# Gated delta rule: output projection with exchanged operands, sums of squares with the squares as the moving operand

## The chip, the cores and the metric

The kernel runs on one core of one Trainium2 chip. The metric is the device time of one execution of the whole program in microseconds (us). TensorE, VectorE, ScalarE, GpSimd and SyncE (which issues the DMAs) each work through a queue of their own and wait for one another by semaphores. In the profile they are called PE (its loads of the stationary operand PEld), DVE, ACT, POOL and SP.

## What is computed

The program is a stack of eight blocks on 2048 tokens of 128 features. The change touches the first alone, the gated delta rule, with 16 heads, keys of 64 and values of 128 features:

```
q, k, v = silu(causal_conv(x @ w_q)), silu(causal_conv(x @ w_k)), silu(causal_conv(x @ w_v))
q = q * rsqrt(sum(q * q, -1) + 1e-6)        # by head; k likewise
beta, g = sigmoid(x @ w_b) * 2.0, -exp(A_log) * softplus(x @ w_a + dt_bias)
def step(S, inp):
    q_t, k_t, v_t, g_t, b_t = inp
    S = S * exp(g_t)
    delta = (v_t - einsum('bhk,bhkv->bhv', k_t, S)) * b_t
    S = S + einsum('bhk,bhv->bhkv', k_t, delta)
    return S, einsum('bhk,bhkv->bhv', q_t * scale, S)
rms = o * rsqrt(mean(o * o, -1) + 1e-5)
y = rms * norm_w * silu(x @ w_g)
out = y.reshape(B, T, 2048) @ w_out
```

Here the batch is 8 sequences (B) of 256 tokens (T). After each block comes a layer norm and the addition to the residual.

## The kernel before

`gated_delta` works on quads: four heads (one group `hg` of NG = 4) of one sequence, 32 in all. A sequence is two chunks (`c`) of 128 tokens. Within a chunk the recurrence is solved in closed form: masked products of keys (`AT`), the inverse of a triangular matrix (`TT`, and `Tm` turned), built from 16 x 16 blocks that GpSimd inverts and that are merged in three levels.

`quads` runs a pipeline of depth four. In each step four quads are in work: x0 is projected and convolved, x1 has its blocks inverted, x2 is merged and solved, x3 gets its gate and output projection. After the first four steps, `Fori` loops over the batch with four steps in its body, so the loop returns every fourth step. The order on each engine is that of its own `step` function, written out by hand.

TensorE's step is: `decays` 0, `turn_y` 0 of x3, `turn_v` 1, first merge level (`merge_y`, L1888, and `merge_t`, L1900), `project` 0, `decays` 1, `out` 0 of x3 (L1981), second `merge_y`, `project` 1, `turn_y` 1, second `merge_t`, `project` 2, `out` 1, third `merge_y`, `merge_t` of chunk 0, `sum_squares` (L1838), `solve` 0 (L1924), `project_gate` 0 (L1914), `turn_k` (L1845), `project` 3 (L1821), `merge_t` of chunk 1, `products` 0 (L1859), `state` (L1940), `outputs` 0 (L1933), `from_state` (L1952), `products` 1, `solve` 1, `project_gate` 1, `turn_v` 0, `outputs` 1.

VectorE's: the masks of the first merge (L2339, L2346), block transposes (L2324, which release the second `merge_y`), `add_y` 0 (L2430), `conv` 0 (L2314), `step_5`, `conv` 1, `turn_64`, `step_6` 0, `conv` 2, `norms` (L2368 to L2378), `add_y` 1, `step_6` 1, `conv` 3, `mask_products` 0, `subtract_memory`, `sum_o`, `mask_products` 1, `turn_16`, `add_o`, which the next first merge waits for.

ScalarE moves the projections out of their banks for the convolutions (`tap3`, L2063), squares q and k (L2083) and scales, copies and gates the rest.

Banks 4 and 5 are shared: `project` n writes bank 4 + n % 2, `turn_y` writes bank 4 and `out` bank 5. So `turn_y` 1 waits for `conv` 0, `out` 1 for `conv` 1, and `project` 3 for `add_y` 1 of the same step. The sums of squares are eight products of 2 columns each, with the squares stationary:

```
i = mm(k.bank[6][:, c * 8 + n * 2:c * 8 + n * 2 + 2], sq[:, n, c * P:(c + 1) * P], halves[:],
       start=True, stop=True)
```

`mm(out, a, b)` keeps `a` stationary and streams the columns of `b`. In the profile's names the moving operand stands first. An fp32 product appears as two records, a transpose as one.

## Time and profile before

| | us |
|---|---|
| median of 3 runs | 5082.28 |
| lowest and highest | 5075.35, 5099.08 |
| the profiled execution, its time | 5070.0 |
| its span | 5068.0 |
| busy in the span: TensorE, VectorE | 4077.8, 3765.4 |
| ScalarE, GpSimd | 2407.9, 2812.8 |

The span runs from the first to the last instruction of the profiled execution. The steps of the gated delta rule fill about the first quarter: their first product on TensorE starts at 45.7 us, the last addition of an output ends at 1382.4 us. The profile's `PEclk` is the clock that TensorE was granted as a share of 2.4 GHz; it is 1.00 or 0.50 (1.2 GHz) at any time, and 0.896 in the mean of the span. An idle stretch in brackets behind a row is that of its own engine, with what ended it.

### The profile page before, as it was taken

Reading aid. Unit: us, or ns where it says so; the run is one execution under the profiler, and the core shown is the slowest. Engines: PE = TensorE matmul, PEld = TensorE weight load, DVE = VectorE, ACT = ScalarE, POOL = GpSimd, SP = SyncE. Lnnn points to the kernel's source line nnn. Section 1 sums busy time; section 2 is a strip of 40 time slices with the busy share of each in tenths; the row PEclk is TensorE's granted clock in tenths of the full one; section 3 lists DMA queues with packets and bytes.
Section 4 is the critical chain, followed back from the end, with each engine's and each line's share of the span. In section 5 each row is a group of like instructions: output and inputs, shape, how many; then the busy total and the mean of one; then the engine's idle time right before and its main releaser. Section 6 shows DMA issues by size and latency. Waiting matters only on the chain. (4 is left out here: it accounts for less than half of the span.)

```text
span 5068.0 us, 74799 instructions
## 1 busy us (share of the span) xinstructions
PE 4077.8 (80%) x19653; PEld 2568.3 (51%) x19773; DVE 3765.4 (74%) x6424; ACT 2407.9 (48%) x4932; POOL 2812.8 (56%) x2705
## 2 busy tenths in 40 slices
PE   5999999999768668667879965688888758888884
PEld 4777777777646546456447742233333323333332
DVE  5676776676567468456138866899999869999995
ACT  3555555555334234222236642566666436666661
POOL 2555555555344144043013330799999529999991
PEclk8999999999877778778999986899999979999997
DMA  1000000000000000000000000000000000000000
GB/s 49 8 8 8 8 8 8 8 7 8 17 0 0 8 13 0 12 1 23 0 17 1 0 13 10 0 0 0 0 0 0 8 0 0 0 0 0 0 0 13
DMA packets 90077, 33.20 MB, mean 7 GB/s; under 512 B 78032, under 2 KB 86112, under 8 KB 88928
## 3 DMA queue, kind: packets, MB, share of 16 engines
q1 hardware_dynamic: 89824, 30.16, 2.5%
q8 instruction: 119, 1.95, 0.2%
q14 instruction: 134, 1.10, 0.1%
HBM read 24.87 MB, written 5.24 MB: 6 GB/s over the span
## 5 line engine op out<-in xcount | busy, mean ns | idle before, releaser
L2970 POOL TENSOR_TENSOR dBx<-dtx,b_row 128x1024 f32<-128x1024 f32 x512 | 1220.4, 2384 | 3.9 <-ACT b_row L2936 3.9
L3004 DVE TENSOR_TENSOR_SCAN h<-banks,dBx 128x1024 f32<-128x1024 f32 x512 | 1168.6, 2283 | 18.1 <-ACT banks L2930 18.1
L2888 PE MATMUL banks<-hc,ident 128*128 128x512 f32 x2048 | 964.6, 594 | 0.0
L2930 ACT ACTIVATE banks<-dt,A 128x510 f32<-128x510 f32 x1024 | 661.7, 682 | 3.6 <-DVE h L3004 3.6
L2936 ACT ACTIVATE b_row<-banks 128x512 f32<-128x512 f32 x512 | 305.9, 597 | 574.1 <-PE banks L2872 574.1
L2888 PEld LDWEIGHTS banks<-hc,ident 128*128 128x128 f32 x2048 | 388.8, 190 | 272.2 <-issue 246.8
L3012 DVE TENSOR_TENSOR hc<-h,banks 128x768 f32<-128x768 f32 x512 | 478.6, 935 | 10.3 <-ACT c_row L2941 6.8
L2872 PE MATMUL banks<-bc_lo,selectors 128*128 128x512 bf16 x1024 | 391.3, 382 | 82.9 <-POOL b_row L2959 73.9
L2979 POOL TENSOR_TENSOR hc<-h,c_row 128x256 f32<-128x256 f32 x512 | 377.0, 736 | 54.5 <-ACT c_row L2941 28.7
L2871 PE MATMUL banks<-bc_hm_c,selectors 128*128 128x512 bf16 x506 | 195.1, 386 | 185.3 <-DVE hc L3012 185.0
L155 POOL MEMSET minus_half<- 128x16 f32 x13 | 1.5, 113 | 520.8 <-POOLq L234 178.8
L2871 PEld LDWEIGHTS banks<-bc_hm_c,selectors 128*128 (+1 forms) x512 | 49.2, 96 | 434.0 <-issue 433.8
L2314 DVE SCALAR_TENSOR_TENSOR v_featmajor<-banks,taps,v_featmajor 128x255 f32<-128x255 f32 (+2 forms) x384 | 167.3, 477 | 130.5 <-ACT v_featmajor L2063 120.0
L2256 POOL TENSOR_TENSOR out_factors<-out_norms,exponents 128x4 f32<-128x4 f32 x64 | 64.5, 1008 | 320.4 <-DVE out_norms L2423 320.4
L821 POOL TENSOR_TENSOR weighted<-probs,f 128x1024 f32<-128x1024 f32 x64 | 120.8, 1904 | 214.8 <-DVE f L872 203.9
L1900 PE MATMUL banks<-inv_turned,steps 128*128 128x64 f32 x1536 | 210.1, 287 | 5.2 <-DVE steps L2339 4.2
L195 PE MATMUL banks<-ident,norm 128*128 128x128 f32 x176 | 45.4, 452 | 209.6 <-DVE norm L165 164.1
L1900 PEld LDWEIGHTS banks<-inv_turned,steps 128*128 128x128 f32 x1536 | 199.2, 203 | 19.5 <-DVE steps L2339 8.7
L1888 PE MATMUL banks<-inv,A_turned 128*128 128x64 f32 x1536 | 188.3, 277 | 24.1 <-issue 19.5
L1888 PEld LDWEIGHTS banks<-inv,A_turned 128*128 128x128 f32 x1536 | 183.2, 196 | 30.9 <-issue 30.9
L2872 PEld LDWEIGHTS banks<-bc_lo,selectors 128*128 (+1 forms) x1024 | 99.6, 97 | 184.0 <-issue 167.0
L2314 DVE SCALAR_TENSOR_TENSOR qk<-banks,taps,qk 128x255 f32<-128x255 f32 (+2 forms) x384 | 167.0, 476 | 23.2 <-ACT qk L2063 12.6
(411 smaller groups left out, 9057.8 us busy)
## 6 DMA issues: line engine op xcount, KB each, us to landing
delta_blocks<-A_turned SPq DMA_DIRECT2D x256, 8.0 KB, 1.5
inv_turned<-delta_blocks SPq DMA_DIRECT2D x256, 8.0 KB, 1.8
blocks<-delta_blocks SPq DMA_DIRECT2D x32, 64.0 KB, 2.1
delta_blocks<-blocks_inv SPq DMA_DIRECT2D x32, 64.0 KB, 1.9
wh<-in_l1f_wh SPq DMA_DIRECT2D x1, 2048.0 KB, 7.6
wqkv<-in_l0f_wqkv SPq DMA_DIRECT2D x2, 768.0 KB, 4.3
residual<-in_x SPq DMA_DIRECT2D x1, 1024.0 KB, 4.7
wv<-in_l0a_wv SPq DMA_DIRECT2D x1, 1024.0 KB, 7.5
```

Source lines behind the costliest of these rows:

```text
L1888: i = mm(k.bank[c][:, h * 64:(h + 1) * 64].rearrange("p (n s) -> p n s", s=s), AT[:, hg, c, h, :], Tm[:, hg % 2, c, h, :].rearrange("p (n ...
L1900: i = mm(k.bank[2 + c][:, h * 64:(h + 1) * 64].rearrange("p (n s) -> p n s", s=s), (step4, step5, step6)[l][:, c, h, :], TT[:, hg % 2, c, ...
L2314: i = stt(out=dst[:, back:], in0=k.bank[4 + n % 2][:, m * T:(m + 1) * T - back], scalar=taps[:, first + m, j:j + 1], in1=dst[:, back:], op ...
L2871: nc.tensor.matmul(k.bank[bank], onto_all(sel[:, 0, bass.ds(n, 1)]), mem[part][:, cols], start=True, stop=False)
L2872: nc.tensor.matmul(k.bank[bank], onto_all(sel[:, which, bass.ds(n, 1)]), mem["lo"][:, cols], start=False, stop=True).then_inc(q[ready], 1)
L2888: i = nc.tensor.matmul(k.bank[e], k.ident[:], hc[:, s, e, :], start=False, stop=False)
L2930: i = nc.scalar.activation(a3[:, :, 1:], d3[:, :, 1:], ACT.Exp, scale=mem["A"][:, e, bass.ds(n, 1)])
L2936: nc.scalar.activation(bsb[:, s, :], k.bank[BBANK], ACT.Copy).then_inc(q["bsb_ready"], 1)
L2970: nc.gpsimd.tensor_tensor(dBx[:, s % NS], dtx[:, :, bass.ds(c * SCH, SCH)], across(bsb[:, s % NS, :], SE), ALU.mult).then_inc(q["dbx_ready ...
L2979: nc.gpsimd.tensor_tensor(hc[:, s % 2, :, DC:], h[:, s % NS, :, DC:], across(csb[:, s % 2, :], SE), ALU.mult).then_inc(q["hcp_ready"], 1)
L3004: v.tensor_tensor_scan(flat(h[:, s % NS]), flat(k.banks[:, at:at + SE, :]), flat(dBx[:, s]), 0.0, ALU.mult, ALU.add).then_inc(q["scanned"], 1)
L3012: v.tensor_tensor(hc[:, s % 2, :, 0:DC], h[:, s, :, 0:DC], across(k.bank[CBANK][:, 0:DC], SE), ALU.mult).then_inc(q["hc_ready"], 1)
```

## The change

1. **Output projection.** `out` runs once a step in place of twice, with `wout` stationary and `yT` of both chunks (256 columns) moving, so it gives features by tokens. It stands where `out` 1 stood. `add_y` runs once and collects the four groups of a sequence in `acc` (128 x 256), the first by a copy.
2. **Back to tokens.** Once a sequence, in the step where x3 is the next sequence's first quad, `turn_out` transposes `acc` in two pieces where `out` 0 stood, and VectorE's `copy_out` puts them into `k.Y`. The memset of `k.Y` goes. After the last step both run once more.
3. **Sums of squares.** Four products with `halves` (now 128 x 4 x 8, a mask of heads) stationary and the squares moving collect 8 x 256 sums in bank 6. ScalarE's `copy_norms` moves them to `ssf`, and `turn_norms` transposes them in two pieces to where they stood before. `turn_norms` stands behind `project_gate` 0.
4. Waits that counted two additions a step count one.

The merge products stay as they are.

TensorE in the loop, around the sums of squares, before (`halves,squares` is `sum_squares`, `v,inv_turned` is `solve`, `wg,x_batch` `project_gate`, `ident,qk` `turn_k`, `norm_featmajor,wv` `project` 3, `inv_turned,steps` `merge_t`):

```order
L1838 MATMUL banks<-halves,squares 128x2 x8
...
L1924 MATMUL banks<-v,inv_turned 128x128 x4
...
L1914 MATMUL banks<-wg,x_batch 128x512
L1845 MATMUL banks<-ident,qk 128x128 x2
L1821 MATMUL banks<-norm_featmajor,wv 128x256 x2
...
L1900 MATMUL banks<-inv_turned,steps_3 128x64 x4
```

and now:

```order
L1843 MATMUL banks<-squares,halves 8x256 x4
...
L1939 MATMUL banks<-v,inv_turned 128x128 x4
...
L1929 MATMUL banks<-wg,x_batch 128x512
L1851 MATMUL banks<-ident,norms_featmajor 128x8 x2
L1857 MATMUL banks<-ident,qk 128x128 x2
L1827 MATMUL banks<-norm_featmajor,wv 128x256 x2
...
L1912 MATMUL banks<-inv_turned,steps_3 128x64 x4
```

The products of 2 columns have become four of 256, and two small transposes stand between `project_gate` and `turn_k`.

TensorE between `decays` 1 and the third `merge_y`, before:

```order
L1829 MATMUL banks<-g_masked,tri 128x512
L1830 MATMUL banks<-hide,ident_bf_3 128x512
...
L1981 MATMUL banks<-wout,y_featmajor 128x128 x4
L1888 MATMUL banks<-inv,A_turned 128x64 x8
L1821 MATMUL banks<-norm_featmajor,wk 128x256 x2
...
L1966 MATMUL banks<-ident,v 128x128 x4
...
L1900 MATMUL banks<-inv_turned,steps_3 128x64 x4
...
L1900 MATMUL banks<-inv_turned,steps_3 128x64 x4
...
L1821 MATMUL banks<-norm_featmajor,wv 128x256 x2
...
L1981 MATMUL banks<-wout,y_featmajor 128x128 x4
L1888 MATMUL banks<-inv,A_turned 128x64 x8
```

and now, in a step without `turn_out`:

```order
L1835 MATMUL banks<-g_masked,tri 128x512
L1836 MATMUL banks<-hide,ident_bf_3 128x512
L1900 MATMUL banks<-inv,A_turned 128x64 x8
L1827 MATMUL banks<-norm_featmajor,wk 128x256 x2
...
L1983 MATMUL banks<-ident,v 128x128 x4
...
L1912 MATMUL banks<-inv_turned,steps_3 128x64 x4
...
L1912 MATMUL banks<-inv_turned,steps_3 128x64 x4
...
L1827 MATMUL banks<-norm_featmajor,wv 128x256 x2
...
L1996 MATMUL banks<-y_featmajor,wout 128x256 x4
L1900 MATMUL banks<-inv,A_turned 128x64 x8
```

The first of the two `out` groups (`wout,y_featmajor`) is gone, and the second streams 256 columns with `wout` stationary.

VectorE around the norms, before:

```order
L2368 TENSOR_SCALAR norms<-banks 128x16
L2370 RECIPROCAL beta_k<-norms 128x8
L2371 RECIPROCAL q_power<-norms 128x8
...
L2375 TENSOR_TENSOR minus_beta_k<-beta_k,minus_beta 128x4
...
L2375 TENSOR_TENSOR minus_beta_k<-beta_k,minus_beta 128x4
L2376 TENSOR_SCALAR q_power<-q_power 128x8
L2378 TENSOR_SCALAR beta_k<-minus_beta_k 128x8
...
L2430 TENSOR_TENSOR block_out<-banks,block_out 128x128
...
L2362 COPY steps_3<-banks 64x4x64
...
L2314 SCALAR_TENSOR_TENSOR v_featmajor<-banks,taps,v_featmajor 128x255 x2
```

and now:

```order
L2401 TENSOR_SCALAR norms<-banks 128x16
L2403 RECIPROCAL beta_k<-norms 128x8
L2404 RECIPROCAL q_power<-norms 128x8
...
L2408 TENSOR_TENSOR minus_beta_k<-beta_k,minus_beta 128x4
...
L2408 TENSOR_TENSOR minus_beta_k<-beta_k,minus_beta 128x4
L2409 TENSOR_SCALAR q_power<-q_power 128x8
L2411 TENSOR_SCALAR beta_k<-minus_beta_k 128x8
L2465 TENSOR_TENSOR batch_out_featmajor<-banks,batch_out_featmajor 128x256
...
L2395 COPY steps_3<-banks 64x4x64
...
L2347 SCALAR_TENSOR_TENSOR v_featmajor<-banks,taps,v_featmajor 128x255 x2
```

The order is the same: the addition of the output stands behind the whole chain of norms, and it is one of 256 columns.

The diff:

```diff
@@ -1690,7 +1690,7 @@
...
     d["l0a_hide"] = f(row > col) * np.float32(-16384)
-    d["l0a_halves"] = f(row // 64 == np.arange(2)[None, :])
+    d["l0a_halves"] = np.concatenate([f(np.arange(8)[None, :] == 2 * n + row // 64) for n in range(4)], 1)
     d["l0a_expo"] = np.tile(np.float32([-0.5] * 4 + [0.5] * 4), (P, 2))
@@ -1714,7 +1714,7 @@
...
         tri, hide, ident = p.sb("tri", [P, 2, P]), p.sb("hide", [P, P], BF16), p.sb("ident_bf16", [P, P], BF16)
-        merge, halves, taps = p.sb("merge", [P, 64]), p.sb("halves", [P, 2]), p.sb("taps", [P, 32, 4])
+        merge, halves, taps = p.sb("merge", [P, 64]), p.sb("halves", [P, 4, 8]), p.sb("taps", [P, 32, 4])
         expo = p.sb("exponents", [P, 2 * 2 * HG])
@@ -1733,11 +1733,13 @@
...
         gate, yT = p.sb("gate", [P, TPB, HG, DV]), p.sb("y_featmajor", [P, TPB, HG, P])
+        ssf = p.sb("norms_featmajor", [8, T])
+        acc = p.sb("batch_out_featmajor", [P, T])
         sqo, os_, of = p.sb("out_squares", [P, HG, DV]), p.sb("out_norms", [P, TPB, HG]), p.sb("out_factors", [P, TPB, HG])
...
                  "xb", "conv", "T16", "Ystep", "TT4", "T32", "T64", "ss", "sp", "AP", "w1", "O1", "osum", "done", "rD", "zeroed",
-                 "inverted", "passed", "passing", "rn", "wd", "y", "there", "back", "through_pe", "through_pool", "through_act", "through_dve")
+                 "inverted", "passed", "passing", "rn", "wd", "y", "yturn", "yout", "ssfm", "sscp", "there", "back", "through_pe", "through_pool", "through_act", "through_dve")
         q = {n: p.sem(n) for n in names}
@@ -1759,6 +1761,9 @@
...
                 step(*[at(B - 1, NG + s - n) if n > s else None for n in range(DEPTH)])
+
+        def first(x):
+            return isinstance(x[1], int) and x[1] == 0
 
@@ -1807,12 +1812,13 @@
...
                     elif n == 1:
-                        wait(pe, "done", 2 * (qa - LAG - 1) + 1)
+                        if hg == NG - 1:
+                            wait(pe, "yout", b)
                     elif n == 2:
...
                     else:
-                        wait(pe, "done", 2 * (qa - LAG))
+                        wait(pe, "done", qa - LAG)
                         wait(pe, "conv", 4 * qa + 2)
@@ -1833,10 +1839,16 @@
...
                     wait(pe, "Dexp", 2 * qa + 2)
+                    for n in range(4):
+                        i = mm(k.bank[6][0:8, 256:512], halves[:, n, :], sq[:, n, :], start=n == 0, stop=n == 3)
+                    i.then_inc(q["ssfm"], 1)
+
+                def turn_norms(a):
+                    qa = a[0]
+                    wait(pe, "sscp", qa + 1)
+                    pe.sem_inc(q["through_pe"], 1)
                     for c in range(TPB):
-                        for n in range(4):
-                            i = mm(k.bank[6][:, c * 8 + n * 2:c * 8 + n * 2 + 2], sq[:, n, c * P:(c + 1) * P], halves[:],
-                                   start=True, stop=True)
+                        i = tr(k.bank[6][:, c * 8:c * 8 + 8], ssf[:, c * P:(c + 1) * P], k.ident[0:8, 0:8])
                     i.then_inc(q["ssps"], 1)
@@ -1908,7 +1920,10 @@
...
                     else:
-                        wait(pe, "yT" if c == 0 else "done", 2 * qe)
+                        if c == 0:
+                            wait(pe, "yT", 2 * qe)
+                        else:
+                            wait(pe, "done", qe)
                     wait(pe, "xb", b + 1)
@@ -1962,24 +1977,33 @@
...
                         wait(pe, "conv", 4 * a[0] + 1)
+                    else:
+                        wait(pe, "yT", 2 * qe + 1)
                     for h in range(HG):
...
 
-                def out(a, e, c):
+                def out(a, x1, e):
                     qe, b, hg = e
-                    wait(pe, "yT", 2 * qe + c + 1)
-                    if c == 0:
+                    wait(pe, "yT", 2 * qe + 2)
+                    if a is not None:
+                        wait(pe, "conv", 4 * a[0] + 2)
+                    else:
                         wait(pe, "gate", 2 * qe + 2)
-                        if a is not None:
-                            wait(pe, "vtok", 2 * a[0] + 2)
-                    else:
-                        wait(pe, "done", 2 * qe + 1)
-                        if a is not None:
-                            wait(pe, "conv", 4 * a[0] + 2)
+                        if x1 is not None:
+                            wait(pe, "vtok", 2 * x1[0] + 2)
                     for h in range(HG):
-                        i = mm(k.bank[5][:, 0:D], yT[:, c, h, :], wout[:, hg * HG + h, :], start=h == 0, stop=h == HG - 1)
+                        i = mm(k.bank[5][:, 0:T].rearrange("p (c t) -> p c t", c=TPB), wout[:, hg * HG + h, :], yT[:, :, h, :],
+                               start=h == 0, stop=h == HG - 1)
                     i.then_inc(q["fin"], 1)
+
+                def turn_out(x1, b):
+                    wait(pe, "done", (b + 1) * NG)
+                    if x1 is not None:
+                        wait(pe, "vtok", 2 * x1[0] + 2)
+                    for t in range(TPB):
+                        i = tr(k.bank[5][:, t * P:(t + 1) * P], acc[:, t * P:(t + 1) * P], k.ident[:])
+                    i.then_inc(q["yturn"], 1)
 
@@ -1996,8 +2020,8 @@
...
                         decays(x0, 1)
-                    if x3:
-                        out(x1, x3, 0)
+                    if x3 and x3[2] == 0 and not first(x3):
+                        turn_out(x1, x3[1] - 1)
                     if x2:
@@ -2011,7 +2035,7 @@
...
                     if x3:
-                        out(x0, x3, 1)
+                        out(x0, x1, x3)
                     if x2:
@@ -2022,6 +2046,7 @@
...
                     if x0:
+                        turn_norms(x0)
                         turn_k(x0)
@@ -2043,6 +2068,7 @@
...
                 quads(pe, step, lambda: pe.wait_ge(q["ready"], 2))
+                turn_out(None, B - 1)
 
@@ -2078,9 +2104,14 @@
...
                     wait(act, "silu_qk", qa + 1)
-                    wait(act, "ssps", qa)
+                    wait(act, "ssfm", qa)
                     x = qk[:, hg].rearrange("p n t -> p (n t)")
                     fn(sq[:].rearrange("p n t -> p (n t)"), x, ACT.Square).then_inc(q["sq"], 1)
+
+                def copy_norms(a):
+                    qa = a[0]
+                    wait(act, "ssfm", qa + 1)
+                    fn(ssf[:], k.bank[6][0:8, 256:512], ACT.Copy).then_inc(q["sscp"], 1)
 
@@ -2172,6 +2203,9 @@
...
                         copy_t(x2, 2, 0)
+                    if x0:
+                        copy_norms(x0)
+                    if x2:
                         scale_z(x2, 0)
@@ -2285,7 +2319,6 @@
...
                 def start():
-                    vv.memset(k.Y[:], 0.0)
                     vv.memset(Tm[:], 0.0)
@@ -2422,12 +2455,20 @@
...
 
-                def add_y(e, c):
+                def add_y(e):
                     qe, b, hg = e
-                    wait(dve, "fin", 2 * qe + c + 1)
+                    wait(dve, "fin", qe + 1)
+                    y = k.bank[5][:, 0:T]
+                    if hg == 0:
+                        i = vv.tensor_copy(acc[:], y)
+                    else:
+                        i = tt(acc[:], y, acc[:], ALU.add)
+                    i.then_inc(q["done"], 1)
+
+                def copy_out(b):
+                    wait(dve, "yturn", b + 1)
                     dve.sem_inc(q["through_dve"], 1)
-                    y = k.Y[:, bass.ds(b * TPB + c, 1), :].rearrange("p a d -> p (a d)")
-                    tt(y, k.bank[5][:, 0:D], y, ALU.add).then_inc(q["done"], 1)
+                    vv.tensor_copy(k.Y[:, bass.ds(b * TPB, TPB), :].rearrange("p a d -> p (a d)"), k.bank[5][:, 0:T]).then_inc(q["yout"], 1)
 
@@ -2442,8 +2483,8 @@
...
                         turn_blocks(x2, "T32")
-                    if x3:
-                        add_y(x3, 0)
+                    if x3 and x3[2] == 0 and not first(x3):
+                        copy_out(x3[1] - 1)
                     if x0:
@@ -2458,7 +2499,7 @@
...
                     if x3:
-                        add_y(x3, 1)
+                        add_y(x3)
                     if x2:
@@ -2475,6 +2516,7 @@
...
                 quads(dve, step, start)
+                copy_out(B - 1)
 
```

## Rows read from the trace of the kernel before

**Rows 1.** Lines view, 162 to 1284 us: group, records | busy us, mean ns | idle us.
```profile
L1838 PE MATMUL banks<-halves,squares 128*128 128x2 f32 x448 | 56.8, 257 | 0.0
```

**Rows 2.** Timeline, TensorE, one step: start us, us, operation, count, [idle before <-releaser].
```profile
906.00 1.97 PE L1888 MATMUL banks<-inv,A_turned 128*128 128x64 f32 x16 [0.86 <-issue]
...
912.86 1.90 PE L1888 MATMUL banks<-inv,A_turned 128*128 128x64 f32 x16
...
916.19 0.66 PE L1966 MATMUL banks<-ident,v 128*128 128x128 f32 x4 [0.51 <-DVE qk L2314]
...
920.23 1.16 PE L1981 MATMUL banks<-wout,y_featmajor 128*128 128x128 f32 x8 [0.50 <-DVE qk L2314]
...
923.85 2.40 PE L1838 MATMUL banks<-halves,squares 128*128 128x2 f32 x16
...
930.10 1.91 PE L1821 MATMUL banks<-norm_featmajor,wv 128*128 x4
931.81 1.05 PE L1900 MATMUL banks<-inv_turned,steps 128*128 128x64 f32 x8
...
945.74 0.52 PE L1888 MATMUL banks<-inv,A_turned 128*128 128x64 f32 x3 [0.85 <-issue]
```

**Rows 3.** Timeline, VectorE, the same step.
```profile
910.70 1.79 DVE L2324 STREAM_TRANSPOSE inv<-inv_turned 32x256 f32<-32x256 f32 x4
913.18 0.29 DVE L2430 TENSOR_TENSOR block_out<-banks,block_out 128x128 f32 x1 [0.69 <-PE banks L1981]
913.38 2.75 DVE L2314 SCALAR_TENSOR_TENSOR qk<-banks,taps,qk 128x255 f32<-128x255 f32 x6
...
926.30 0.17 DVE L2368 TENSOR_SCALAR norms<-banks 128x16 f32<-128x16 f32 x1 [0.81 <-PE banks L1838]
...
927.61 0.29 DVE L2430 TENSOR_TENSOR block_out<-banks,block_out 128x128 f32 x1
...
933.01 2.76 DVE L2314 SCALAR_TENSOR_TENSOR v_featmajor<-banks,taps,v_featmajor 128x255 f32<-128x255 f32 x6 [4.65 <-ACT v_featmajor L2063]
```

**Rows 4.** Timeline, all engines, the step before it.
```profile
864.89 1.97 PE L1888 MATMUL banks<-inv,A_turned 128*128 128x64 f32 x16 [0.86 <-issue]
...
873.74 1.12 PE L1981 MATMUL banks<-wout,y_featmajor 128*128 128x128 f32 x8
...
885.69 1.90 PE L1838 MATMUL banks<-halves,squares 128*128 128x2 f32 x16
...
889.24 1.87 PE L1914 MATMUL banks<-wg,x_batch 128*128 128x512 f32 x2
...
891.17 1.03 PE L1821 MATMUL banks<-norm_featmajor,wv 128*128 x4
...
893.26 2.77 DVE L2314 SCALAR_TENSOR_TENSOR v_featmajor<-banks,taps,v_featmajor 128x255 f32<-128x255 f32 x6 [3.57 <-ACT v_featmajor L2063]
```

**Rows 5.** Windows view: stretch, busy by engine, then granted clock, DMA share, GB/s.
```profile
884.00:887.00 3.00, 3.00 (x29) 3.00 (x29) 2.71 (x7) 1.50 (x3) 1.72 (x2) 1.00 0.13 25
887.60:890.80 3.20, 3.20 (x10) 2.21 (x11) 1.70 (x9) 1.14 (x4) 0.00 (x0) 0.50 0.16 15
925.20:931.80 6.60, 6.60 (x21) 5.11 (x22) 1.99 (x10) 1.53 (x5) 3.57 (x4) 0.50 0.16 20
867.20:873.80 6.60, 6.60 (x22) 4.93 (x22) 3.19 (x9) 1.75 (x3) 4.84 (x10) 0.50 0.00 0
3150.80:3160.60 9.80, 9.80 (x12) 3.32 (x10) 0.00 (x0) 1.97 (x1) 0.00 (x0) 0.50 0.00 0
```

**Rows 6.** Timeline, ScalarE: the copy of 256 columns out of a bank.
```profile
930.35 0.38 ACT L2093 ACTIVATE k_tokens<-banks 128x256 f32<-128x256 f32 x1 [0.88 <-PE banks L1845]
```

**Rows 7.** Timeline, VectorE, ahead of the first step.
```profile
37.84 1.76 DVE L2288 MEMSET block_out<- 128x2048 f32 x1 [0.83 <-PEq L2491]
```

**Rows 8.** Timeline, TensorE, at a return of the loop.
```profile
983.58 2.05 PE L1829 MATMUL banks<-g_masked,tri 128*128 128x512 f32 x2 [3.03 <-issue]
```

**Rows 9.** Timeline, TensorE, the last projection of the block.
```profile
1379.91 2.07 PE L1981 MATMUL banks<-wout,y_featmajor 128*128 128x128 f32 x8 [0.69 <-ACT y_featmajor L2152]
```

## The prediction

> **What bounds the kernel now.** The change touches only the gated delta rule, so I read, in this order, the lines of its steady stretch, the timeline of two of its steps on TensorE and VectorE, and the granted clock beside them. Between 162 and 1284 us the sums of squares have 448 records, 16 a step, so 28 steps take 1122 us, 40.07 us each [rows 1].
>
> One step can be cut at three places: the first merge product (L1888), the sums of squares (L1838), and the fourth convolution on VectorE (L2314 after its wait for ScalarE), up to the next first merge.
> - In the step of [rows 2, 3] these lie at 906.00, 923.85, 933.01 and 945.74: 17.85 + 9.16 + 12.73 = 39.74 us.
> - In the step before it [rows 4] at 864.89, 885.69, 893.26 and (first row of [rows 2]) 906.00: 20.80 + 7.57 + 12.74 = 41.11 us.
>
> The last part is the same in both, because VectorE works through it without a pause (masks, memory, norms, block transposes, outputs) and TensorE waits for its end. The two other parts differ by TensorE's clock, and the clock falls at two places:
> - **Drop S**, right behind the sums of squares. From 884 to 887 us TensorE is busy 3.00 of 3.00 us at full clock, from 887.6 to 890.8 it runs at 0.50; a step later 0.50 reaches from 925.2 to 931.8 [rows 5]. In the 28 steps I count 20 of the short kind and 8 of the long. The long one costs 9.16 - 7.57 = 1.59 us more. Sixteen passes of 2 columns stand directly ahead of it.
> - **Drop M**, behind the first merge (867.2 to 873.8 at 0.50, [rows 5]), in 7 of the 28. TensorE idles 0.86 us ahead of L1888 [rows 4] and then runs passes of 64 columns. It costs 20.80 - 17.85 = 2.95 us.
>
> Every fourth step also idles 3.03 us at the loop's return [rows 8]. The check: 20 x 38.16 + 8 x 39.74 + 7 x 2.95 + 7 x 3.03 = 1123 us against 1122. (38.16 is 17.85 + 7.57 + 12.74.) TensorE and VectorE hand the step to each other; neither is alone the bound.
>
> **The change part by part.** Records of one group overlap the next by 0.16 us, so a pass of 256 columns costs (1.03 - 0.16)/4 = 0.22 us (L1821, [rows 4]), one of 2 columns (1.90 - 0.14)/16 = 0.11 (L1838, [rows 4]), one of 128 (1.16 - 0.16)/8 = 0.125 (L1981, [rows 2]). An fp32 product is two passes.
>
> *Columns.* Sums of squares: 16 x 0.11 = 1.76 before, 8 x 0.22 = 1.76 after. Output projection: 2 x 8 x 0.125 = 2.0 before, 8 x 0.22 = 1.76 after. Added: two small transposes a step and two large ones every fourth. Four transposes take 0.66 us (L1966, [rows 2]), so at most 0.33 us a step and 0.33 every fourth. TensorE's own work does not shrink; what can change is the clock and the waits.
>
> *First part, first merge to squares.* The first `out` and its `add_y` leave. Now VectorE stands 0.69 us for that `out`, adds, and starts convolution 0 at 913.38; without it, it starts when the block transposes end, 910.70 + 1.79 = 912.5 [rows 3]. TensorE's next merge waits for the same transposes, so it gains 912.86 - 912.5 = 0.36 only. The two stops at 916.19 and 920.23 are waits for convolutions 0 and 1 [rows 2] and move 0.88 earlier. The one `out` left then takes 1.76 in place of 1.00, so the squares start 0.88 - 0.76 = 0.1 us earlier: **17.75**. With drop M the block transposes are no limit (TensorE came to L1981 at 873.74), all behind them moves by 1.0 more for the removed `out`, and the part takes about 19.8 in place of 20.80.
>
> *Second part, squares to convolution 3.* Here a wait is added. After the squares (1.76) TensorE does `solve` and `project_gate`, which took until 889.24 + 1.87 - 0.16 = 890.95, 3.50 us, at half clock [rows 4], so 1.75 at full. ScalarE's copy of 8 x 256 (0.38 as the copy of 128 x 256, [rows 6]; between 0.2 and 0.6) is hidden by them. It is queued ahead of `scale_z`, which waits for `solve` anyway. Then `turn_norms` 0.33, landing 0.2, the norms chain on VectorE 927.61 - 926.30 = 1.31, and behind it `add_y` [rows 3]. One 128 x 256 addition lies between one and two of 0.29; I take 0.43. `project` 3 may overwrite bank 5 only after `add_y`: 1.76 + 1.75 + 0.33 + 0.2 + 1.31 + 0.43 + 0.05 = 5.8 us after the squares' start. Before it began at 891.17 - 885.69 = 5.48 [rows 4], with the norms long done. From `project` 3 to convolution 3 it is 893.26 - 891.17 = 2.09. So **7.9 us** if the clock stays full, against 7.57 (short drop) and 9.16 (long). What drop S gives back, the later norms take: TensorE idles some 1.9 us ahead of `project` 3.
>
> *Third part:* nothing moved, **12.73**, all VectorE.
>
> *Once:* the memset of 1.76 us leaves the start [rows 7], bounds 0 and 2.1 (with the pause behind it). At the end the last `out` ran at half clock, 2.07 - 0.16 = 1.9 us [rows 9]; it becomes 8 x 0.44 = 3.5, and an addition, two transposes and a copy follow, 0.4 to 1.5 us: +2 to +3. Together +1. The copy and transposes of each batch stand where TensorE waits for the block transposes; their 0.4 on VectorE every fourth step is up to +3.
>
> *Sum.* A step without drop M: 17.75 + 7.9 + 12.73 = 38.4. Against 38.16: 20 x 0.24 = +5. Against 39.74: 8 x 1.34 = -11. Drop M costs 2.05 in place of 2.95: 7 x 0.9 = -6. Once and batches: +1 to +3, less in the first four steps. **-12 + 2 = -10 us**, with -20 and +5 as bounds from the unsure terms. The profiled execution has a span of 5068.0 and a time of 5070.0, so it would become 5060; the median of the runs shown lies 12 above it, so I forecast 5072.
>
> **The rivals.**
> - *S stays* (slower; also the case in which the change does not do what it says). Busy is not enough to hold the clock: from 3150.8 to 3160.6 TensorE is busy 9.80 of 9.80 us at 0.50, on products of 8 rows (L2718, [rows 5]). The new products use 8 of 128 stationary columns. For the drop's end speaks that all 128 rows stream 256 columns. If it stays, `turn_norms` ends 1.76 + 3.50 + 0.33 = 5.6 after the squares, `project` 3 starts at 7.6, convolution 3 at 9.7: +2.0 in each of 20 steps, about +0.9 in 8 (the long one still slows `project` 3), -6 for drop M: +41 us, **5123**. It decides from the point where the drop stays in more than 5 or 6 of the 28 steps (10 us / 1.8).
> - *New drop* (slower or even). The new idle stretch, 1.9 us with only four transposes just ahead of it, is longer than the 0.86 us that goes with drop M, though wide passes surround it. If the clock falls there, merges, products and state run half speed, 1.3 to 1.7 us a hit; or drop M meets more steps, 2.05 a hit. In 14 to 28 steps +20 to +42: **5100**. The Trainium skill ("TensorE: Matmul & The Clock Gate", Part 4, PE-mode transpose) says that transposes do not count as TensorE activity in the same way; no run here separates that, and it would speak for this case.
> - *No drops at all* (faster). Drop M follows the same idle stretch as before, but its phase moves with the step's length; it came in 7 of 28 steps. Should it vanish, 7 x 2.05 = -14 more, and with the low ends of the copy and the addition: **5052**. The Trainium skill ("TensorE: Matmul & The Clock Gate", Why this matters for your kernels) has the rule that the clock stays up while TensorE is kept continuously busy. By that rule there would be no drop after 884 to 887, which the trace contradicts: busy 3.00 of 3.00, then 0.50.
>
> **How the numbers follow.** Forecast 5072, chance 35%, own range 5057 to 5085. S stays 28%, 5105 to 5135. New drop 20%, 5090 to 5112. No drops 17%, 5040 to 5058. Over or under 0.5% (25 us, about what a measurement of this kernel tells from none) begins at 5057 and 5108. Faster: most of "no drops" and 5 of the forecast, 0.18. Slower: 25 of "S stays" and 7 of "new drop", 0.32. Same: 0.50. The range that leaves out one in ten at each side: 5045 to 5128.
>
> **What would show it.** The clock at 1.00 behind the squares and their block at 1.8 us; `solve` and `project_gate` about 1.8 us together; VectorE's norms about 4 us after the squares' start; TensorE idle about 1.9 us ahead of `project` 3, released by VectorE's addition; convolution 0 directly behind the block transposes; steps of 38.4 us in place of 38.2 and 39.7. The forecast is wrong if the clock still falls behind the squares, if it falls behind the idle stretch, or if `project` 3 does not wait.

## The result, and the profile after

| | before | after |
|---|---|---|
| median of 7 runs, us | 5079.07 | 5122.43 |
| lowest and highest | 5064.55, 5099.08 | 5114.43, 5140.91 |
| profiled execution, span | 5068.0 | 5139.0 |

The ratio is 1.0093 (95% interval 1.0072 to 1.0115): the change makes the kernel slower by 37 to 58 us. The forecast was 5072 us, a change too small to tell. The profiled execution of after is the slowest of the seven, 18.5 us above their median, and that of before lies 9 below its own, so the two traces are 71 us apart and the medians 43. The counts of steps below come from that slowest execution, whose mean granted clock is 0.897 against 0.900 to 0.907 in the other six, so these may hold fewer stretches at half clock.

Where the 71 us came from, in the two traces: the first sums of squares start 2.6 us earlier, the 31 steps up to the last sums take 65.2 us more (1290.6 against 1225.4), what follows them up to the layer norm takes 15.4 more, and the other seven blocks 7 less.

TensorE's timeline of after (start us, us, operation, count, idle before and its releaser), two steps one behind the other; this answers to [rows 2, 4]:

```profile
888.45 1.89 PE L1900 MATMUL banks<-inv,A_turned 128*128 128x64 f32 x16
890.18 1.06 PE L1912 MATMUL banks<-inv_turned,steps 128*128 128x64 f32 x8
891.16 1.89 PE L1843 MATMUL banks<-squares,halves 128*8 128x256 f32 x8
892.99 1.16 PE L1939 MATMUL banks<-v,inv_turned 128*128 128x128 f32 x8
893.98 1.02 PE L1929 MATMUL banks<-wg,x_batch 128*128 128x512 f32 x2
894.94 0.28 PE L1851 MATMUL banks<-ident,norms_featmajor 8*128 8x8 f32 x2
895.15 0.44 PE L1857 MATMUL banks<-ident,qk 128*128 128x128 f32 x2
897.68 0.67 PE L1827 MATMUL banks<-norm_featmajor,wv 128*128 x2 [2.09 <-DVE batch_out_featmajor L2465]
...
930.63 1.89 PE L1843 MATMUL banks<-squares,halves 128*8 128x256 f32 x8
...
937.15 1.62 PE L1827 MATMUL banks<-norm_featmajor,wv 128*128 x4 [2.09 <-DVE batch_out_featmajor L2465]
938.55 1.81 PE L1912 MATMUL banks<-inv_turned,steps 128*128 128x64 f32 x8
940.29 2.08 PE L1871 MATMUL banks<-qk 64*128 64x256 f32 x8
942.30 2.07 PE L1955 MATMUL banks<-weighted,k_tokens 128*128 128x256 f32 x4
944.17 1.18 PE L1948 MATMUL banks<-v,QK_turned 128*128 128x128 f32 x8
```

The windows view of these two steps (the stretch, its length, busy by engine PE, PEld, DVE, ACT, POOL, then granted clock, DMA share, GB/s), which answers to [rows 5]. The first two rows are of the first step, the others of the second:

```profile
884.00:887.00 3.00, 2.49 (x17) 2.01 (x17) 2.82 (x7) 2.33 (x5) 1.98 (x7) 1.00 0.04 11
891.20:893.00 1.80, 1.80 (x10) 0.61 (x9) 1.44 (x4) 0.38 (x1) 1.44 (x4) 1.00 0.00 0
930.60:937.20 6.60, 4.51 (x24) 2.31 (x23) 3.60 (x13) 2.28 (x7) 4.58 (x7) 1.00 0.13 18
937.80:944.20 6.40, 6.40 (x24) 4.92 (x23) 4.18 (x12) 1.71 (x4) 1.29 (x1) 0.50 0.00 0
944.60:947.00 2.40, 2.40 (x31) 2.21 (x29) 0.15 (x1) 2.07 (x5) 0.00 (x0) 1.00 0.00 0
```

Drop S (the fall of the clock right behind the sums of squares) is gone: from the squares to `project` 3 the clock stays at 1.00, and their block takes 1.83 us (892.99 - 891.16). In its place the clock falls *behind the idle stretch*: TensorE waits 2.09 us for VectorE's `add_y`, and then merges, products and state run 6.4 us at 0.50, the state product 2.07 us in place of 1.1. The step before had the same 2.09 us of idle (897.68) and kept its clock. In the 28 steps from the first merge at 143.7 us I count the new drop in 17: in each of the first seven, then in every second one. Six of the 17 are all the steps in which the loop returns; there the idle stretch is 2.3 to 2.4 us, elsewhere 2.07 to 2.14. A step with the new drop mostly takes 42.5 us, at a loop's return 46.0 to 46.8; a step without any drop takes 39.25 to 39.4. Drop M (behind the first merge) is left in three of the 28. Before, the 28 steps took 1122 us; now they take 1185.

The stretch that `project` 3 waits for, all engines but TensorE; it answers to the norms and `add_y` of [rows 3]:

```profile
895.26 0.17 DVE L2401 TENSOR_SCALAR norms<-banks 128x16 f32<-128x16 f32 x1 [2.55 <-PE banks L1851]
...
895.72 1.04 POOL L2283 TENSOR_TENSOR weighted<-v,decay_to_end 128x512 f32<-128x512 f32 x1 [1.50 <-ACT v L2154]
895.96 0.89 DVE L2408 TENSOR_TENSOR minus_beta_k<-beta_k,minus_beta 128x4 f32<-128x4 f32 x2 [0.17 <-issue]
896.72 2.91 POOL L2275 TENSOR_TENSOR norm_powers<-norms,exponents 128x16 f32<-128x16 f32 x1
...
897.12 0.42 DVE L2465 TENSOR_TENSOR batch_out_featmajor<-banks,batch_out_featmajor 128x256 f32<-128x256 f32 x1
```

`norms` takes 1.86 us up to `add_y`; before it took 1.31 [rows 3]. Two products of 128x4 (L2408) take 0.89 us together. The first starts while `weighted` runs on GpSimd, takes 0.81 us and ends with it (896.77 against 896.76); the second takes 0.15. `norms` has no wait for GpSimd in the kernel. Of the 64 such products in the block, 25 take 0.73 to 0.96 us beside `weighted` and two more 1.08 and 1.10 beside GpSimd's `g_masked` (128x512); 32 of the rest take 0.15 to 0.16, and five take 0.24 to 0.29, each to the end of a `g_masked`.

Behind the last sums of squares two stretches at 0.50 appear while the pipeline drains. The last projection runs at half clock, as before [rows 9]. The windows of those stretches:

```profile
1371.20:1391.40 20.20, 17.36 (x75) 16.69 (x76) 6.22 (x17) 3.52 (x9) 11.23 (x34) 0.50 0.02 4
1408.80:1429.00 20.20, 17.71 (x78) 17.11 (x79) 6.44 (x17) 2.56 (x5) 3.52 (x4) 0.50 0.00 1
```

### The profile page after: what moved, and what is told of

Same layout as the page of the kernel before. It is cut to its first block and busy times, and to the rows that moved or that the text cites. A ratio compares the mean times of both kernels' runs of the same rounds, so it can differ in the third digit from the quotient of the medians.

```text
span 5139.0 us, 73943 instructions
## 1 busy us (share of the span) xinstructions
PE 4085.7 (80%) x19341; PEld 2515.7 (49%) x19341; DVE 3782.0 (74%) x6399; ACT 2418.7 (47%) x4964; POOL 2810.4 (55%) x2705
## 5 line engine op out<-in xcount | busy, mean ns | idle before, releaser
L2913 PE MATMUL banks<-bc_hm_b,selectors 128*128 128x512 bf16 x512 | 196.4, 384 | 77.5 <-POOL b_row L3001 73.4
L1912 PE MATMUL banks<-inv_turned,steps 128*128 128x64 f32 x1536 | 221.5, 297 | 6.4 <-DVE steps L2372 4.5
L1912 PEld LDWEIGHTS banks<-inv_turned,steps 128*128 128x128 f32 x1536 | 211.4, 213 | 20.7 <-DVE steps L2372 8.5
```

The costliest lines, as they stand in the source:

```text
L1912: i = mm(k.bank[2 + c][:, h * 64:(h + 1) * 64].rearrange("p (n s) -> p n s", s=s), (step4, step5, step6)[l][:, c, h, :], TT[:, hg % 2, c, ...
L2913: nc.tensor.matmul(k.bank[bank], onto_all(sel[:, 0, bass.ds(n, 1)]), mem[part][:, cols], start=True, stop=False)
```

## The experiments

The first four separate the halves of the change and its wait. Each is compared with before on the same chip; the ratios carry 95% intervals. The diffs show the lines that matter, and `...` stands for lines left out.

**squares_only.** The kernel before with the new sums of squares (`sum_squares`, `copy_norms`, `turn_norms`); `out` and `add_y` stay in two parts.

```diff
+                    for n in range(4):
+                        i = mm(k.bank[6][0:8, 256:512], halves[:, n, :], sq[:, n, :], start=n == 0, stop=n == 3)
...
```

> The kernel before with the streamed sums of squares alone (copy and transposes of the norms included); the output projection stays in its two parts. Theory A (the later norms hold project 3 and the idle stretch ahead of it brings a new drop of the clock): squares to project 3 about 6.4 us, no drop behind the squares, a new drop behind project 3 in a third to half of the steps and in those with the loop's return; time 5110 to 5130, as much slower as the whole change. Rival B (the exchanged output projection is what costs): time 5070 to 5085.

Measured: 5129.01 us, ratio 1.0114 (1.0088 to 1.0139). Two rows of its TensorE timeline, and the window behind the second:

```profile
509.35 1.10 PE L1822 MATMUL banks<-norm_featmajor,wv 128*128 x4 [2.70 <-DVE block_out L2446]
...
924.26 1.75 PE L1822 MATMUL banks<-norm_featmajor,wv 128*128 x4 [2.02 <-DVE block_out L2446]
```

```profile
924.80:931.60 6.80, 6.80 (x25) 5.24 (x25) 4.32 (x12) 1.71 (x4) 1.46 (x1) 0.52 0.02 3
```

`project` 3 starts 6.44 to 7.1 us after the squares, behind 2.01 to 2.70 us of idle, and the new drop comes in 11 of 28 steps. Behind the longest stretch, 2.70 us (509.35), it does not come: `project` 3 then takes 1.10 us, as at full clock. Of the six steps in which the loop returns three have it, where all were expected. So the squares alone bring the whole loss.

**out_only.** The change with the sums of squares of before.

```diff
-                    for n in range(4):
-                        i = mm(k.bank[6][0:8, 256:512], halves[:, n, :], sq[:, n, :], start=n == 0, stop=n == 3)
...
                     for c in range(TPB):
-                        i = tr(k.bank[6][:, c * 8:c * 8 + 8], ssf[:, c * P:(c + 1) * P], k.ident[0:8, 0:8])
+                        for n in range(4):
+                            i = mm(k.bank[6][:, c * 8 + n * 2:c * 8 + n * 2 + 2], sq[:, n, c * P:(c + 1) * P], halves[:],
+                                   start=True, stop=True)
```

> The changed kernel with the sums of squares as before; the exchanged output projection, collected by sequence and turned, alone. Theory A: squares to project 3 stays 5.0 to 6.2 us and the drop behind the squares stays; the part from the first merge to the squares is unchanged at 17.9 us without a drop, 20.0 in place of 20.8 with one; time 5070 to 5085, same as before. Rival B: 5100 to 5130.

Measured: 5064.7 us, ratio 0.9975 (0.9959 to 0.9992): a small gain, 5 us below the range that was expected. Drop S stays in most steps. In six of 28 it does not come, and three of these take 36.6 us:

```profile
1042.54 1.90 PE L1843 MATMUL banks<-halves,squares 128*128 128x2 f32 x16
...
1046.40 1.10 PE L1826 MATMUL banks<-norm_featmajor,wv 128*128 x4
```

`project` 3 then follows 3.86 us after the squares and waits for nothing. The first part of a step takes 17.84 us, and mostly 20.0 to 20.15 with drop M: forecast 17.75 and 19.8.

**filled_idle.** The change with products that nobody reads between `turn_k` and `project` 3.

```diff
+                def fill(e):
+                    if e is not None:
+                        for n in range(4):
+                            mm(k.bank[2][:, 0:256], k.ident[:], wq[:, n * 256:(n + 1) * 256], start=True, stop=True)
...
                         turn_k(x0)
+                        fill(x2)
                         project(x0, 3)
```

> The changed kernel with four products of 256 columns on constant operands between turn_k and project 3, 1.8 us at full clock; nothing reads them. They fill TensorE's idle stretch of 2.1 us and change no wait. Theory A: the new drop vanishes, steps take 39.3 us throughout except at the loop's return (43 in place of 46) and where the clock falls behind the first merge; time 5070 to 5090, 35 to 50 us below the changed kernel though TensorE does more. Rival C (the idle stretch is not the cause of the new drop): the drop stays in about half of the steps, time 5115 to 5140.

Measured: 5076.42 us, ratio 1.0001 (0.9986 to 1.0016). TensorE's timeline, and two windows on either side of `project` 3:

```profile
897.56 1.89 PE L1857 MATMUL banks<-wq,ident 128*128 128x256 f32 x8
899.81 1.10 PE L1827 MATMUL banks<-norm_featmajor,wv 128*128 x4 [0.36 <-DVE batch_out_featmajor L2471]
```

```profile
893.30:899.80 6.50, 6.15 (x31) 3.65 (x31) 3.50 (x13) 2.28 (x7) 4.44 (x6) 1.00 0.13 18
899.80:907.00 7.20, 6.61 (x52) 5.65 (x54) 5.27 (x16) 4.38 (x9) 1.95 (x1) 1.00 0.03 4
```

`project` 3 still starts 6.5 us after the squares, but the clock falls behind it in no step. Work without a use gives back 46 us (5122.43 - 5076.42; ratios 1.0093 and 1.0001). Together with the two runs that take the idle stretch away or shorten it and add no product (add_and_step_first and weighted_later, below), this shows that without the idle stretch the new drop does not come. It does not show that the stretch is enough: 11 of the 28 steps of after have it and keep their clock.

**add_and_step_first.** The change with `add_y` and `step_6` 1 ahead of `norms` on VectorE.

```diff
-                        norms(x0)
                     if x3:
                         add_y(x3)
                     if x2:
                         step_6(x2, 1)
                     if x0:
+                        norms(x0)
                         conv(x0, 3)
```

> The changed kernel with VectorE's order turned: the addition of the output and the last step_6 ahead of the norms. Theory A: project 3 starts 4.3 us after the squares in place of 6.5, TensorE does not idle ahead of it, no new drop there; steps without a drop take 37.1 to 37.6 us in place of 39.3, and the time is 5010 to 5045, faster than both kernels. Rival C (the new drop comes from the narrow stationary operand of the squares or from the small transposes, not from the idle stretch): project 3 starts earlier, but the clock still falls within 5 us behind the squares in about half of the steps; time 5050 to 5085.

Measured: 5004.06 us, ratio 0.9862 (0.9836 to 0.9889), a little under what was expected, and 70 us faster than the kernel before. TensorE's timeline and a window:

```profile
881.39 1.89 PE L1843 MATMUL banks<-squares,halves 128*8 128x256 f32 x8
...
885.38 0.44 PE L1857 MATMUL banks<-ident,qk 128*128 128x128 f32 x2
885.66 1.03 PE L1827 MATMUL banks<-norm_featmajor,wv 128*128 x4
```

```profile
881.40:888.00 6.60, 6.60 (x41) 4.42 (x41) 4.13 (x14) 3.47 (x10) 4.55 (x6) 1.00 0.14 19
```

TensorE is busy all the way; `project` 3 starts 4.27 us after the squares. The small transposes still stand ahead of it, and the clock holds. Steps without a drop take 36.9 to 37.2 us (up to 37.4 after a loop's return), and only four of 28 have drop M. Convolution 3 could not start earlier in any case: VectorE waits 0.26 us for ScalarE there. What the norms lost by going last costs nothing.

Four more runs ask how much of this is the order alone, which of the two pieces matters, and what else makes the norms late.

**order_only.** The kernel before with the same turn of the order, its squares unchanged.

```diff
-                        norms(x0)
                     if x3:
                         add_y(x3, 1)
                     if x2:
                         step_6(x2, 1)
                     if x0:
+                        norms(x0)
                         conv(x0, 3)
```

> The kernel before with the second addition and step_6 ahead of the norms, nothing else. Theory A (the order matters only where the norms come late): the drop behind the squares stays, squares to project 3 5.0 to 6.2 us as before, time 5065 to 5085. Rival E (the gain of the turned order is its own, with or without streamed squares): 5010 to 5040.

Measured: 5073.15 us, ratio 1.0009 (0.9988 to 1.0029). There the norms and `add_y` are both done before TensorE comes to `project` 3 (`add_y` ends at 927.90, `project` 3 starts at 930.10 in [rows 2, 3]), so TensorE waits for neither and the order is worth nothing.

**squares_and_order.** squares_only with the order of order_only.

> The kernel before with the streamed sums of squares, and with the second addition of the output and step_6 ahead of the norms; the output projection stays in two parts. Theory A: project 3 4.3 us after the squares, no drop behind the squares nor behind project 3, steps without a drop 36.9 to 37.2 us, time 5000 to 5020; the exchanged output projection then is worth 0 to 10 us. Rival B (the exchanged projection carries part of the gain): 5025 to 5050.

Measured: 5007.37 us, ratio 0.9872 (0.9847 to 0.9897). The four kernels form a table: with the old squares the order is worth 0.1%, with the new ones 2.4%; the new squares are worth +1.1% in the old order and -1.4% in the turned one. Beside the new squares, the exchanged output projection adds nothing that the intervals separate.

**add_first.** The change with `add_y` alone ahead of `norms`.

```diff
-                        norms(x0)
                     if x3:
                         add_y(x3)
+                    if x0:
+                        norms(x0)
                     if x2:
                         step_6(x2, 1)
```

> The changed kernel with only the addition of the output ahead of the norms; step_6 of the second chunk stays behind them. Theory A: project 3 starts 4.3 us after the squares, as with both moved; the idle stretch moves behind project 3, ahead of the last merge, and is 1.0 to 1.5 us; steps without a drop take 37.3 to 38.0 us, the time is 5010 to 5045. Rival D (step_6, not the addition, is what holds TensorE): project 3 at 6.5 us and 5110 to 5130.

Measured: 5088.71 us, ratio 1.0029 (1.0012 to 1.0047). The expectation missed: this lies 44 us above its range. Its timeline, TensorE and then VectorE, and a window of the same step:

```profile
892.78 1.03 PE L1827 MATMUL banks<-norm_featmajor,wv 128*128 x4
895.14 1.10 PE L1912 MATMUL banks<-inv_turned,steps 128*128 128x64 f32 x8 [1.34 <-DVE steps L2395]
```

```profile
892.61 0.17 DVE L2401 TENSOR_SCALAR norms<-banks 128x16 f32<-128x16 f32 x1 [2.22 <-PE banks L1851]
...
894.58 0.43 DVE L2395 COPY steps<-banks 64x256 f32<-64x256 f32 x1
```

```profile
896.50:899.80 3.30, 3.30 (x12) 2.21 (x9) 2.76 (x9) 0.16 (x1) 0.47 (x1) 0.50 0.00 0
```

`project` 3 starts 4.27 us after the squares, as meant. But `step_6` 1 stands behind the norms, and TensorE's last `merge_t` waits for it: 1.34 us of idle, one place further on. The third part of a step grows from 12.7 to 14.0 us or more, the drop-free step is 38.5 to 38.7 us where 37.3 to 38.0 was expected, and drop M comes in 10 of 28 steps. The clock also falls behind the idle stretch in its new place, in 7 of 28 steps and for about 3.4 us each (the row at 896.50). Both products of VectorE that TensorE waits for have to go ahead of the late norms.

**turn_norms_earlier.** The change with `turn_norms` between `solve` and `project_gate`.

```diff
                         solve(x2, 0)
+                    if x0:
+                        turn_norms(x0)
+                    if x2:
                         project_gate(x0, x2, 0)
                     if x0:
-                        turn_norms(x0)
                         turn_k(x0)
```

> The changed kernel with the two small transposes of the norms ahead of project_gate 0 in place of behind it, so that the norms land 0.9 us earlier; VectorE's order as in the change. Theory A: project 3 at 5.5 to 5.7 us after the squares, the idle stretch ahead of it 1.1 to 1.3 us, steps without a drop 38.3 to 38.5 us, and the new drop in fewer steps or none: time 5040 to 5080. Rival C (an idle stretch of any length there brings the drop): still in a third to half of the steps, 5085 to 5105.

Measured: 5049.25 us, ratio 0.9966 (0.9953 to 0.998), inside the range. TensorE's timeline, in a step in which the loop returns and in one in which it does not:

```profile
480.07 1.10 PE L1827 MATMUL banks<-norm_featmajor,wv 128*128 x4 [2.14 <-DVE batch_out_featmajor L2465]
...
917.92 1.10 PE L1827 MATMUL banks<-norm_featmajor,wv 128*128 x4 [0.57 <-DVE batch_out_featmajor L2467]
```

In the second step `project` 3 starts 5.04 us after the squares, behind 0.57 us of idle, less than the 5.5 to 5.7 and 1.1 to 1.3 expected: the two products of 128x4 fall ahead of `weighted` and take 0.30 together. In the six steps in which the loop returns they meet another GpSimd product: there the first ends with `g_masked`, after 0.94 to 1.02 us in five of them, and `project` 3 waits 2.13 to 2.21 us. The new drop comes in one of these six, and in no other step. So an idle stretch as long as that of after need not bring it.

**weighted_later.** The change with GpSimd's `weighted` behind `norm_powers`; nothing is moved on TensorE or VectorE.

```diff
+                    if x1:
+                        norm_powers(x1)
                     if x3:
                         weigh(x3)
-                    if x1:
-                        norm_powers(x1)
```

> The change as it is, with GpSimd's product `weighted` moved behind its `norm_powers` (only the order of these two on GpSimd). In the change one of the two 128x4 multiplies of `norms` (L2408) takes 0.73 to 0.96 us where `weighted` runs and ends beside it, 0.15 otherwise. Theory A, the multiply waits for the end of `weighted`: with it gone both multiplies take 0.15, `norms` 1.3 us in place of 1.86, `project` 3 starts 5.8 to 5.95 us after the squares in place of 6.50, and a step without a drop takes 38.6 to 38.8. TensorE's idle ahead of `project` 3 is then 1.4 to 1.6 us in place of 2.1. If the clock still falls behind it in every second step, the time is 5100 to 5110 us; if the shorter idle holds the clock, 5055 to 5085, which would say that the late norms and their length alone decide on the new drop. Theory B, the multiply is slow because of `norm_powers` itself or of something else: multiplies and steps stay, 5115 to 5130. A `weighted` that lands too late for the state product would show as an idle of TensorE ahead of it and add to either.

Measured: 5070.93 us, ratio 0.9994 (0.9978 to 1.001), as Theory A had it. All engines but TensorE, then TensorE, then a window:

```profile
889.84 2.90 POOL L2275 TENSOR_TENSOR norm_powers<-norms,exponents 128x16 f32<-128x16 f32 x1 [3.78 <-DVE norms L2401]
...
890.19 0.30 DVE L2408 TENSOR_TENSOR minus_beta_k<-beta_k,minus_beta 128x4 f32<-128x4 f32 x2 [0.17 <-issue]
```

```profile
891.28 1.10 PE L1827 MATMUL banks<-norm_featmajor,wv 128*128 x4 [1.48 <-DVE batch_out_featmajor L2465]
```

```profile
891.20:898.00 6.80, 6.13 (x50) 5.20 (x50) 4.87 (x14) 3.97 (x9) 2.55 (x2) 1.00 0.00 0
```

The lines view of 162 to 1284 us, after and then this kernel:

```profile
L2408 DVE TENSOR_TENSOR minus_beta_k<-beta_k,minus_beta 128x4 f32<-128x4 f32 x54 | 21.3, 432 | 4.5 <-issue 4.4
```

```profile
L2408 DVE TENSOR_TENSOR minus_beta_k<-beta_k,minus_beta 128x4 f32<-128x4 f32 x56 | 8.3, 165 | 4.6 <-issue 4.6
```

`project` 3 starts 5.90 us after the squares, a step without a drop takes 38.6 to 38.9, the idle is 1.48 us, and behind it the clock falls in no step. Drop M remains in 9 of 28. So 0.6 us in a wait decides on 50 us in the kernel: 28 x 0.6 = 17 are the wait itself, the rest is the clock.

## Why the prediction was wrong

*The first part was right*, within 0.2 us a step: 17.93 us against 17.75, and 20.1 to 20.3 with drop M against 19.8 (three steps). Convolution 0 starts directly behind the block transposes.

*Drop S was right.* It is gone in every steady step of after, squares_only and their kin. "S stays" gave 5123 us for a mechanism that is nowhere in the trace of after; that the measured time lies on it is chance.

*The second part failed twice.* The forecast had 5.8 us from the squares to `project` 3 and 1.9 us of idle. Measured are 6.52 and 2.09. Its terms against the rows of the step at 891.16: squares 1.83 for 1.76; `solve` and `project_gate` 1.95 for 1.75; `turn_norms` and its landing 0.32 for 0.53; norms 1.86 for 1.31; `add_y` 0.42 for 0.43; from there to `project` 3 0.14 for 0.05. The landing of 0.2 had no row behind it; with the transposes it came out 0.21 smaller. Of the 0.7 us of error 0.55 is the norms. I took their 1.31 us (926.30 to 927.61, [rows 3]) from a stretch in which `weighted` was not beside them, and moved them to where it is. In the step of [rows 3] GpSimd's `weighted` starts 2.1 us after their end:

```profile
929.73 1.04 POOL L2249 TENSOR_TENSOR weighted<-v,decay_to_end 128x512 f32<-128x512 f32 x1 [3.03 <-ACT v L2123]
```

Moving `weighted` away gives 5.90 us, steps of 38.7 and 3 us less than before on the same chip, next to the forecast's 5.8, 38.4 and 10 less. That the time comes so close is in part luck: the steps are 0.3 us longer than forecast and drop M comes in 9 of 28, while a return of the loop costs less, 1.9 us (a step without a drop, in filled_idle) and not 3.03. The 3.03 is TensorE's idle stretch; in the kernel before the clock also falls at each of its six returns.

*The step that failed is the idle stretch: the sum priced it at its own length and put nothing for the clock.* TensorE idles 1.9 us in the forecast, the second part is 7.9 us "if the clock stays full", and the third part stays 12.73. What came is the rival "new drop". It had 20%, 1.3 to 1.7 us a hit and 5100 us. It came in 17 of 28 steps, at 3.1 us a hit (42.46 - 39.34) and 5.1 at a loop's return (46.3 - 41.2). The rival named merges, products and state as what runs at half speed, but its price has no working. The row at 937.80 shows 6.4 us at 0.50 without a pause, so 3.2 us are lost on TensorE, and the step loses nearly all of it, because products and state then feed VectorE late: the third part, which I had as 12.73 us of VectorE alone, mostly takes 15.4 to 15.7 in such a step. The 5.1 at a loop's return holds a second, shorter fall of the clock at the return itself, which the kernel before has there too. The sum of the 28 steps (six returns of the loop; the prediction counted seven): 28 x 39.33 + 6 x 1.9 at the loop's returns + 35 for 11 hits + 6 x 5.1 + 3 x 2.3 for drop M = 1185 us. The terms are means of the same trace, so this divides the time up and tests nothing. Against before, the longer wait is 28 x 0.7 (39.33 against a mean of 38.6), +20; the new drops are +66, the loop's returns -7 and the rarer drop M -14: together +65, where the two traces differ by 63.

*The warning stood in the same text.* It named 0.86 us of idle as what goes with drop M. An idle stretch more than twice as long as one that already comes with a drop needed a price of its own in the forecast, not in a rival. How many steps it would hit could not be read from before. The rule of the Trainium skill on transposes ("TensorE: Matmul & The Clock Gate", Part 4, PE-mode transpose), which the prediction set behind this rival, stays undecided: filled_idle adds products and takes idle away at once. The transposes alone do not bring the drop; add_and_step_first has the same four and no idle stretch, and keeps its clock there.

*The ends.* The memset's part was right in sign and too small: the first squares start 2.6 us earlier, 1.76 was forecast with 2.1 as its bound. They start as early in out_only (56.44 us) and as late as before in squares_only (59.13 us), which keeps the memset. The last `out` with its copy costs 3.05 us more from the last transposes of y to the layer norm (7.68 against 4.63), as forecast (+2 to +3). The other 12.4 us behind the last squares were not in the sum; two stretches of 20.5 us at half clock stand there, for one of 23.9 before. Why there are two, no run here says.

*Open.* Why the clock falls behind some of these idle stretches and not behind others. In after the same idle brought a drop in each of the first seven steps and later in every second one; in squares_only the longest stretch, 2.70 us, brought none; in turn_norms_earlier 2.13 to 2.21 us brought one in six. The length of the stretch alone does not decide.

## What to carry over

When a change puts a round trip through another engine into a chain, list what stands in that engine's queue ahead of the result that is waited for, and put the waited-for pieces first: here moving one call behind two others was worth 2.3% to 2.4%, and without it the change lost. Take the duration of a small operation from a place with the same neighbours on GpSimd as its new one. And price an idle stretch of TensorE by the work that may follow it at half clock, not by its own length.

## What the runs showed of the hardware

**A small VectorE product waits for a GpSimd one.** A 128x4 product of two operands takes 0.15 to 0.165 us alone and, where it starts beside GpSimd's 128x512 `weighted`, 0.73 to 0.96, and it ends with it. The Trainium skill ("SBUF — State Buffer", SBUF: two separate sides) states it: the two engines share a pair of ports as an exclusive lock, held for a whole instruction, and a VectorE instruction with two SBUF inputs needs it against a GpSimd instruction that reads SBUF. The trace agrees for `weighted`, and for `g_masked` (1.08 and 1.10 us in after). It does not for `norm_powers`, also a GpSimd operation on two operands in SBUF (a power, 128x16, 2.9 us): beside it, in weighted_later, 59 of 64 products of VectorE take 0.149 to 0.164 us.

**The clock came back late.** After the idle stretch the clock stays at 0.50 while TensorE is busy 6.40 of 6.40 us, which is where the price of 3.1 us comes from. Ahead of `project` 3, 2.0 to 2.6 us of idle brought it in many steps, the longest stretch of 2.70 us did not, and the 1.48 us of weighted_later did in none of 28. Yet 1.29 to 1.52 us of idle ahead of the last merge of add_first was followed by 0.50 in 7 of 28 steps, so 1.48 us is no length that is safe.

**A narrow stationary operand kept full clock.** The new products fill 8 of 128 stationary columns, with 256 moving ones, and run at 1.00 (the row at 891.20), where the old ones with 2 moving columns were followed by 0.50. The products of 8 rows later in the program run at 0.50 in the stretch shown in [rows 5]; why these do and the new ones do not, no run here separates.
